# A state scan in which TensorE multiplies v and B itself, GpSimd makes all products with C, and the running sum moves a stage ahead

## The reference, cut to what matters

```
delta = softplus(dt_proj(x_dt) + bias)         # step size per channel and pixel
h_n[l] = exp(-A_n * delta[l]) * h_n[l-1] + (delta[l] * x[l]) * B_n[l]
y[l]   = sum over n of C_n[l] * h_n[l]
```

## Time and profile before

| | us |
|---|---|
| median of 3 runs | 2945.18 |
| lowest and highest run | 2942.47, 2949.40 |
| span of the profiled execution, first to last instruction | 2938.3 |
| from the start of `l0_steps` to the start of `l0_scan` | 119 to 280 |
| first scan of `l0_scan` to the start of its last | 301.8 to 1971.9 |
| DVE, POOL, PE, ACT busy in the whole span | 85%, 65%, 77%, 59% |

### The profile page before, as it was taken

How to read it: one execution, slowest core, us unless ns; L and a number is a source line. 1 busy time by engine, 2 the same in 40 slices (tenths; PEclk the granted TensorE clock), 3 DMA queues, 4 the chain that set the end, 5 groups by cost and what they waited for, 6 DMA issues and landing times. The chain is left out here.

```text
span 2938.3 us, 27688 instructions
## 1 busy us (share of the span) xinstructions
PE 2263.7 (77%) x8714; PEld 1197.9 (41%) x8714; DVE 2503.6 (85%) x2085; ACT 1743.5 (59%) x2935; POOL 1896.0 (65%) x646
## 2 busy tenths in 40 slices
PE   6853677777877777787777778778984999799579
PEld 3421234343443434343443434444442555355444
DVE  5657999999999999999999999986787777699721
ACT  1566787878888888888878788863230000263220
POOL 0166999999999999999999999984000000198000
PEclk9967799999999999999999999998997999899689
DMA  1277445555454555545455554535005453100360
GB/s 48 88 219 272 102 112 137 130 124 130 115 133 118 131 136 123 129 112 132 119 131 134 125 129 112 135 90 191 0 0 143 110 129 104 43 8 8 82 89 24
DMA packets 145457, 323.07 MB, mean 110 GB/s; under 512 B 48219, under 2 KB 63840, under 8 KB 140320
## 3 DMA queue, kind: packets, MB, share of 16 engines
q1 hardware_dynamic: 144224, 317.17, 42.7%
q10 hardware_dynamic: 1088, 4.13, 0.6%
HBM read 234.46 MB, written 46.87 MB: 96 GB/s over the span
## 5 line engine op out<-in xcount | busy, mean ns | idle before, releaser
L903 POOL TENSOR_TENSOR l0c_r<-l0c_r,l0c_v 128x1536 f32<-128x1536 f32 x253 | 869.4, 3442 | 96.3 <-DVE l0c_r L862 96.3
L940 ACT ACTIVATE ps<-l0c_dlt,l0c_na 128x512 f32<-128x512 f32 (+1 forms) x1152 | 625.5, 574 | 286.5 <-DVE l0c_h L891 267.2
L912 POOL TENSOR_TENSOR l0c_hcp<-l0c_cb,l0c_h 128x1536 f32<-128x1536 f32 x216 | 743.2, 3446 | 5.5 <-DVE l0c_h L891 4.1
L891 DVE TENSOR_TENSOR_SCAN l0c_h<-ps,l0c_h,l0c_r 128x768 f32<-128x768 f32 x384 | 694.1, 1808 | 1.8 <-issue 1.2
L818 PE MATMUL ps<-l0c_hcp,net_ident 128*128 128x512 f32 x1728 | 645.2, 496 | 25.2 <-ACT l_Z L933 11.9
L950 ACT ACTIVATE l0c_r<-l0c_S,l0c_floor,l0c_na 128x768 f32<-128x768 f32 x576 | 579.9, 1014 | 0.1
L862 DVE SCALAR_TENSOR_TENSOR l0c_r<-l0c_r,ps 128x768 f32<-128x768 f32 x576 | 536.1, 931 | 18.1 <-issue 8.5
L752 PE MATMUL ps<-l0c_Bp,l0c_sel 96*128 96x512 bf16 x1012 | 256.0, 335 | 301.1 <-DVE l0c_hcv L869 146.1
L818 PEld LDWEIGHTS ps<-l0c_hcp,net_ident 128*128 128x128 f32 x1728 | 299.2, 193 | 297.6 <-issue 216.9
L891 DVE TENSOR_TENSOR_SCAN l0c_h<-ps,l0c_r 128x768 f32<-128x768 f32 x192 | 335.4, 1747 | 0.0
L1628 PE MATMUL ps<-l_prod,l_wa 128*96 128x384 f32 (+1 forms) x888 | 292.1, 493 | 25.7 <-DVE l_prod L1545 25.7
(11 more groups left out here) (280 smaller groups left out, 2739.9 us busy)
## 6 DMA issues: line engine op xcount, KB each, us to landing
l0c_cb<-cf SPq DMA_DIRECT2D x432, 384.0 KB, 5.5
l_other<-l_p SPq DMA_DIRECT2D x22, 864.0 KB, 6.0
dlt<-l0s_dl SPq DMA_DIRECT2D x36, 384.0 KB, 2.3
v<-l0s_vv SPq DMA_DIRECT2D x36, 384.0 KB, 2.9
l0c_dlt<-dlt SPq DMA_DIRECT2D x36, 384.0 KB, 3.6
l0c_v<-v SPq DMA_DIRECT2D x36, 384.0 KB, 4.4
l_other<-l_p SPq DMA_DIRECT2D x22, 288.0 KB, 6.7
l0c_Bp<-bc SPq DMA_DIRECT2D x36, 144.0 KB, 3.8
```

The lines of the kernel that those rows point to most:

```text
L891: dve.tensor_tensor_scan(h[:, n, :], da[j % 2], r[:, j % NR, :], init, ALU.mult, ALU.add).then_inc(s_scan, 1)
L903: pool.tensor_tensor(two, two, v[:, (j // N) % 2, :].unsqueeze(1).to_broadcast([128, 2, SEG]), ALU.mult).then_inc(s_w, 2)
L912: pool.tensor_tensor(hcp[:, p % NHP:p % NHP + 2, :], cb[:, p % NCB:p % NCB + 2, :], h[:, e % N:e % N + 2, :], ALU.mult).then_inc(s_hp, 2)
L940: act.activation(da[e % 2][:, part], dlt[:, i, part], ACT.Exp, scale=na[:, i, n:n + 1]).then_inc(done, 1)
```

## The change

The order of units changes: the tile is now the inner loop, so that the three tiles share the B of one direction and segment. A step is now one state of 64 channels and two states side by side: rows 0 to 63 hold state 2g and rows 64 to 127 state 2g+1 of the same 64 channels, and `s` tells which half of the tile's channels. There are still 576 steps of 128 x 768.

- v*B is made by PE alone: `turn` transposes v (stationary, four matmuls, three parts per unit), ACT copies it out of PSUM (`empty`, EMPTY), POOL builds diagonal images of B (`image`, one for each 3 steps, 192 in all), and `v_b` multiplies them in 24 matmuls of 64 x 64 x 64 in f32. The result fills both banks of PB, and there is one such buffer. `b_r` runs one step ahead of the scan, not four.
- POOL's product with v and DVE's product with C are gone. POOL makes all products with C, 288 instructions of 128 x 1536.
- S is computed in `l0_steps` (`running_sum` on DVE, 36 scans), stored to DRAM and loaded like `dlt`, twice each, so that both halves of the partitions have it.
- ACT saves the last column of each scan (`carry`), since only three pairs of h are kept.
- The bf16 parts, their casts and their 24 stores are gone. B is made directly in transposed form, C in one matmul group per chunk.

The core of the diff:

```diff
@@ l0_steps, vector
+            def running_sum(i, idle):
+                if i % UN:
+                    dve.wait_ge(s_sum, i)
+                    init = So[:, (i - 1) % ND, SEG - 1:SEG]
...
+                dve.tensor_tensor_scan(So[:, i % ND, :], dl[:, i % ND, :], idle, init, ALU.add, ALU.bypass
+                                       ).then_inc(s_sum, 1)
...
                     dve.wait_ge(s_q, i)
+                    if i >= 2:
+                        running_sum(i - 2, ln)
@@ l0_steps, sync
+                if i == NC // 2 + 3:
+                    sp.wait_ge(s_bce, NC)
+                    for r in range(K * B):
+                        k, b = divmod(r, B)
+                        sp.dma_start(d["cf"][k, 3 * b:3 * b + 3, :, :].rearrange("r n l -> n r l"),
+                                     cr[N * r:N * r + N, :].unsqueeze(1).to_broadcast([N, 3, L])).then_inc(s_out, 16)
@@ l0_scan
-        NR, NHV, NHP, NCB = 8, 3, 4, 4
-        AHEAD, LATE, LAG = 4, 5, 6
-        BY_VECTOR = ((2, 5, 10, 13),)
-        SP, PART, TURN, EMPTY = 12, SEG // 2, (7, 9), (14, 15)
+        G = N // 2
+        NR, NH, NHP, NG, NI = 6, 3, 3, 3, 11
+        LATE, LAG = 5, 4
+        TURN, EMPTY, STORE = (5, 7, 9), (11, 13, 15), LAG + 6
@@ tensor
+            def v_b(j):
+                u, n = divmod(j, N)
+                g, s = divmod(n, 2)
+                q = image_of(j)
+                pe.wait_ge(s_vt, 3 * u + 3)
+                pe.wait_ge(s_img, q + 1)
                 if j:
+                    pe.wait_ge(s_r, j)
+                for c in range(6):
+                    for half in range(2):
+                        rows = slice(64 * half, 64 * half + 64)
+                        o = PB[half] + 64 * (5 - c if place(u)[1] % 2 else c)
+                        for x in range(2):
+                            mm = pe.matmul(ps[64 * x:64 * x + 64, o:o + 64], vT[rows, u % 2, c, 64 * s:64 * s + 64],
+                                           img[rows, q % NI, x, c, :], start=True, stop=True)
+                mm.then_inc(s_vb, 1)
+
+            def turn(u, part):
+                if part == 0:
+                    pe.wait_ge(s_v, 16 * (u + 1))
+                if u or part:
+                    pe.wait_ge(s_vt, 3 * u + part)
...
+            for j in range(J + LATE):
+                u, n = divmod(j, N)
+                if n in TURN and u + 1 < U:
+                    turn(u + 1, TURN.index(n))
+                if j + 1 < J:
+                    v_b(j + 1)
+                if j >= LATE and (j - LATE) % 2:
+                    add_y((j - LATE) // 2)
@@ vector
+            b_r(0)
             for j in range(J):
...
+                if j + 1 < J:
+                    b_r(j + 1)
...
+                dve.tensor_tensor_scan(h[:, j // 2 % NH, s, :], da[j % 2], r[:, j % NR, :], init, ALU.mult, ALU.add
                                        ).then_inc(s_scan, 1)
@@ gpsimd
+            for p in range(J // 2):
+                ks, at = divmod(p, T * G)
+                times_c(p)
+                if G <= at < G + 5:
+                    image(2 * G * ks + at + 3)
+                elif at >= G + 5 and ks + 1 < K * NSEG:
+                    image(2 * G * (ks + 1) + at - G - 5)
@@ scalar
+            def empty(u, part):
+                act.wait_ge(s_turn, 3 * u + part + 1)
...
+                    if e and e % 2 == 0:
+                        carry(e // 2 - 1)
                 if n in EMPTY and u + 1 < U:
                     empty(u + 1, EMPTY.index(n))
-                if n == FIRST and 0 < u < U:
+                if n == STORE and 0 < u < U:
                     store(u - 1)
```

More of the change, by code:

```diff
@@ L634, in l0_scan @@
-        s_ds, s_dsum = sem("ds"), sem("dsum")
-        s_turn, s_vt, s_vb = sem("turn"), sem("vt"), sem("vb")
-        s_own, s_shared, s_tanh, s_w, s_b, s_c, s_S, s_init = map(
-            sem, ("own", "shared", "tanh", "w", "b", "c", "S", "init"))
-        PB, PC, PY = 0, SEG, 3 * BANK
+        s_v = sem("v")
+        s_cb = [sem(f"cb{i}") for i in range(NG)]
+        s_scan, s_r, s_hc, s_y, s_evac, s_last = map(sem, ("scan", "r", "hc", "y", "evac", "last"))
+        s_ds, s_dsum, s_init, s_places = map(sem, ("ds", "dsum", "init", "places"))
@@ new lines, in turn @@
+            def turn(u, part):
[3 more added lines that the diff above has]
+                    pe.wait_ge(s_vt, 3 * u + part)
+                for c in range(2):
+                    for x in range(2):
+                        mm = pe.matmul(ps[64 * x:64 * x + 64, PV + 128 * c:PV + 128 * c + 128],
+                                       halves(v[:, :])[:, x, 2 * part + c, :], ident[:, :], start=True, stop=True)
+                mm.then_inc(s_turn, 1)
@@ new lines, in add_y @@
+            def add_y(p):
+                u, g = divmod(p, G)
+                if g == 0 and u:
+                    pe.wait_ge(s_evac, u)
+                pe.wait_ge(s_hc, p + 1)
+                for lo, hi in pieces(PY):
+                    for s in range(2):
+                        mm = pe.matmul(ps[64 * s:64 * s + 64, lo:hi], places[:, 0, :], hc[:, p % NHP, s, lo - PY:hi - PY],
+                                       start=(g == 0), stop=(g == G - 1))
+                mm.then_inc(s_y, 1)
+                if place(u)[1] and 2 <= g < 2 + len(y_pieces(u)):
+                    lo, hi, src = y_pieces(u)[g - 2]
+                    pe.matmul(ps[:, lo:hi], ident[:, :], src, start=False, stop=False)
@@ L837, in _ @@
+            pe.wait_ge(s_places, 16)
+            for part in range(3):
+                turn(0, part)
+            v_b(0)
+            for j in range(J + LATE):
+                u, n = divmod(j, N)
+                if n in TURN and u + 1 < U:
[4 more added lines that the diff above has]
+                    add_y((j - LATE) // 2)
         @block.vector
@@ L906, in times_c @@
[L906 to L920 removed]
+            pool.wait_ge(s_places, 16)
@@ L922, in _ @@
+            for q in range(NI):
+                image(q)
+            for p in range(J // 2):
+                ks, at = divmod(p, T * G)
[4 more added lines that the diff above has]
+                    image(2 * G * (ks + 1) + at - G - 5)
         @block.scalar
@@ L977, in _ @@
-            FIRST, LAST = LAG + LATE, N - 1
+                act.activation(r[:, j % NR, :], S[:, u % 2, n % 2, :], ACT.Tanh, bias=floor[:, :],
+                               scale=na[:, 1, column(j)]).then_inc(s_tanh, 1)
+            def empty(u, part):
+                act.wait_ge(s_turn, 3 * u + part + 1)
+                if u >= 2 and part == 0:
+                    act.wait_ge(s_vb, (u - 1) * N)
+                act.activation(vT[:, u % 2, 2 * part:2 * part + 2, :].rearrange("p c x -> p (c x)"), ps[:, PV:PV + 256],
+                               ACT.Copy).then_inc(s_vt, 1)
@@ L978, in _, with carry @@
+            def carry(p):
+                act.wait_ge(s_scan, 2 * p + 2)
+                act.activation(last[:, place(p // G)[0], p % G, :], h[:, p % NH, :, SEG - 1], ACT.Copy
+                               ).then_inc(s_last, 1)
+            for part in range(3):
+                empty(0, part)
             act.wait_ge(s_in[0], 16 * NLOAD)
```

566 lines of the change are left out of this document (205 added, 361 removed).

## The result

The changed kernel takes 3272.06 us (median of 4 runs, 3264.01 to 3295.39), the kernel before 2947.29 in the same session: a ratio of 1.111, 95% interval 1.107 to 1.115. It is slower, as forecast, but by 325 us and not by 75; 3272 lies far outside 2955 to 3150. The profiled execution has a span of 3269.4 us, 331 more than before.

A forecast was written before the change was run, and what follows sets the result against it. In the scan DVE, back to back, was taken as the bound, with POOL also full. The terms -203 + 249 - 8 + 28 + 9 = +75 gave span 3013 and time 3020 us, range 2955 to 3150.

The forecast's parts named there:

- the clock term: Scan: PE idles twice a unit and may run at 1.2 GHz; 0.25 us per second stall, +9 us.
- the price of add_y: Scan, after each second v_b: four matmuls take 0.75 us if they overlap, 1.5 if not; hidden.
- DMA in the scan: Scan: loads at 173 GB/s come in time; 0, at worst 2 us x 12 units.
- DVE's list: Scan: products with C and the running sum leave DVE, 5.64 us less a unit, -203 us if DVE never waits.
- v_b: Scan: PE's new product before each b_r takes 1.36 us with signals and fits the 1.58 us of room.
- Rival 1: Scan: TensorE becomes the bound if small tiles don't overlap; 3250 us, chance 0.13.
- turn and empty: Scan: PE, ACT and DVE wait in turn at v_b(8) and v_b(10); 7.11 us a unit, +249 us.
- The store: Scan: add_y's wait for ACT's store is covered by the longer wait of turn part 1; 0.
- rival 3: Scan, middle tile: the loads starve POOL; +24 us and more, 3045 us, chance 0.07.
- Step sizes: Stage before the scan: DVE's added running sum, C and B copies, C transfers; 175 against 147 us, +28.
- Start: Ahead of the first scan: about 3 us after the first b_r instead of 8.6, one running sum less; -8 us.
- Rival 2: Scan: the stall isn't there and the store's wait shows; -114 us, 2831 us, chance 0.07.

The follow-up runs named there:

- e9: Changed kernel with copies and store moved, loads one at a time, pieces behind the next v*B, C rows spread, B batches one to a unit: 2842.62 us.
- e12: e9 with the loads of S and step sizes in eight halves over six pairs of C loads: 2808.28 us.
- e1: Changed kernel with ScalarE's three copies of turned v two steps earlier: 3078.45 us.
- e6: e3 with the pieces of the sum so far put behind the v*B of the next step: 2935.53 us.
- e2: Changed kernel with ScalarE's store of the previous unit's sum two steps earlier, copies unmoved: 3241.62 us.
- e10: Changed kernel with only the loads of S and the step sizes issued one at a time: 3240.65 us.
- e8: e3 with the eight batches of turned B in the step-size stage one to a unit instead of two: 2940.5 us.
- e7: e3 with the eight C-row transfers of the step-size stage spread over every second unit: 2949.14 us.
- e3: Changed kernel with ScalarE's copies and its store both two steps earlier: 2964.98 us.

## Why the prediction was wrong

Between the two profiled executions there are 331 us: 51 ahead of the first scan, 277 in the scan, 3 behind it. Forecast were 20, 55 and 0.

In short, the direction and the place of the stall were right; the terms beside the chain failed. Of the 222 us that the scan is over the forecast, the steps 8 and 10 have 46, step 12 has 76, steps 6 and 7 have 60, and some 40 are spread over the other steps and a floor slightly above the forecast one. The steps of the prediction that failed are the clock term, the price of add_y with its pieces, and the 0 for DMA in the scan.

*DVE's list, -203:* right. The floor of a unit came out at 41.1 us against 40.80, and in e9 11 of the first 35 units take under 42 us.

*v_b:* right that it fits, and the price was 0.93 us at 2.4 GHz, below the 1.19 (1.36 with the signals) that I took. That it came so near is luck. My 0.041 us were read from rows that count records, two to a matmul, so 48 of them would have been 2.0 us. What made up for it is that four quarters of the array work at once and not two column ranges: in the trace four records start within 26 ns of each other, then the next four. Rival 1, TensorE as the bound, is out: in e12 PE is busy for 1125 us of 1550 and b_r stands at the floor in most steps. The 62 ns a matmul that I quoted from the Trainium skill, TensorE: Matmul & The Clock Gate, section Wait — 56ns, not 53.3ns?, don't bind here either: 24 matmuls took 0.93 us.

*turn and empty, +249:* **the chain was right.** At 2.4 GHz the second stall measures 5.78 to 5.81 less 2.57, 3.2 us, the 3.20 of the text. But the links were not: the copy took 0.36 us (0.44 in the text), turn 0.66 (0.26, again by records), v_b with its signals 1.0 (1.30), and these errors cancel. At part 1 ScalarE's lateness of 0.71 us did not show (its copy starts 1.20 us behind the scan in the median, 1.06 at part 2); something else stood there, see the store.

**What failed first is the clock term, +9.** I had put 0.25 us for each second stall. In the changed kernel v_b(10) started at 1.2 GHz in 23 of 35 units (6.88 against 5.78 us), v_b(8) in 26 (7.39 against 6.30): my estimate from these is 53 us. With the clock the steps 8 and 10 cost 304 us where 258 were forecast. And the half clock outlasts the stall: it makes the product sum and piece behind it 2.83 + 1.96 us long, which v_b(12) then waits for. Step 12 cost 76 us, forecast 0; with the copies moved 50 of them are gone (e1), and the other 26 are the piece (e6).

**Second, add_y at 0.75 us.** The step reads "two matmuls took 645.2 / 864 = 0.75 us; now four". The count in that row is of records, two for each f32 matmul; 864 is the number of single matmuls. Four of them, in pairs that overlap, are 1.5 us, and 1.51 was measured. I had that value as the case without overlap and judged it harmless because its 0.2 us stay within a spare of 0.22. That is true at 2.4 GHz in a step without a piece, and nowhere else. The pieces of the sum so far (L823 before, L770 now) I hadn't costed at all in their new place.

*The store, 0, covered by the turn's wait:* **wrong, and again by the price of add_y.** In the changed kernel the product sum that waits for the store took 2.83 us in the median, at 1.2 GHz, and turn part 1 started 0.47 us after the copy was complete (medians of 34 units): add_y held n = 8, not the copy. By my estimate 1.51 us would have been covered. Moving the store alone was worth 31 us (e2). With the copy moved instead (e1), n = 8 is 4.2 us above the floor, where I had 1.9: besides the 2.83 us for 0.75, that sum left out turn itself, 1.07 us.

*DMA in the scan, 0:* **wrong, and by an unlisted mechanism.** I checked whether POOL and the loads come in time, which they do; "starve POOL" (rival 3) didn't happen. What came late was TensorE's own code, four times as much as before. Most of the 3.88 us at n = 6 and of n = 7 is that: of 60 us above the floor, e10 took 46 away, and its time fell by 31; with the stalls gone it was 63. The page of before has the instruction queue at 1.16 MB, and the diff says 24 matmuls for each state and segment; the product was there to be made.

*Step sizes, +28:* measured +54 (L552, which answers to L546, goes from 125.6 to 326.5 us, 200.9 against 147.1). The 4.43 us a unit was right (4.4), and the 8.0 for the C units (7.5 to 8.2). Wrong were the four units of B at 5.0, taken from ScalarE: TensorE sets them at 11.4, 13.8, 9.1 and 7.3. A batch of 54 small f32 matmuls is 108 records, and at 1.2 GHz 216 took 11.74 us, 5.9 a batch; two batches go to a unit (one to a unit brought the first scan 9.9 us forward, e8). And the eight C transfers cost 11.5 us of waiting, not 7 (e7 brought it 5.8 us forward).

*Start, -8:* from the end of that stage to the first scan it is 26.8 us where it was 27.2, and the stage begins 1.9 us earlier: -2. What I had counted is there: the first scan comes 3.7 us behind the first b_r, where it was 8.6. But the first b_r comes 4.5 us later behind that stage: the first load of the scan stage is issued 8.8 us behind the last L552, where it was 6.0, and between them lies the running sum of the last unit, which I had only taken off; the other 1.7 us stay open.

*Rival 2, faster:* its condition was right as a statement. It needed stalls under 2.5 us. In e3 they are 1.1 at n = 8 and 0.2 at n = 10, and the time is 2965, not 2831, because its sum had nothing for the waits for code and the pieces, and too little for B batches and C rows. With those mended too (e12) it is 2808.

## What to carry to other kernels

Where a queue with a fixed order waits for an engine whose wait is behind the very work that it should feed, look for the latest place at which the producer is ready and the earliest at which the consumer needs it, and put the step there: here four numbers were worth 307 us. Price a stall with the half clock on everything that stands behind it until the waiting is made up, not on the stalled operation alone. When an edit multiplies an engine's instructions, read its instruction queue in the profile and keep bursts of loads out of the way of its code.

## What I hadn't expected of the chip

- One f32 matmul is two records, one bf16 matmul is one: 576 x 24 f32 matmuls gave x27648. A price from "busy over count" is that of half a matmul.
- Four 64 x 64 quarters of the array work at once: 48 records in 0.93 us at 2.4 GHz, 1.56 at 1.2 GHz; four start within 26 ns, and the next four some 60 ns behind the first.
- TensorE stood still for up to 4.9 us in the middle of a run of matmuls when its next 16 KB of code came late, most often while the DMA engines were full (share 0.95 to 1.05 around the gap shown). It went on 2.6 to 3.1 us after the packet had started, and took one each 6.4 us (median in e3).
- The same v_b took 1.7 times as long at 1.2 GHz, and add_y 1.9 times.
